# Dictionary setup moved between convolution rounds, and a group norm with one averaging matmul instead of two

## The reference

```
x = x + conv3x3_circular(_gn(x), weight)          # 64 -> 64 channels, written with an FFT
x = x + recon(_gn(x), dictionary)                 # 1024 x 512 dictionary

D = dictionary / (norm of each column + 1e-10)
X = 4x4 patches of all 64 channels                # 1024 numbers a patch, 1024 patches an image
G = D^T D + 1e-5 I;  h_bar = (D^T X)^T;  h = h_bar
for k in 1..5:                                    # greedy pursuit, per patch
    index = argmax |h| over atoms not yet chosen
    extend the Cholesky factor L with G[I, index]
    x_stack = solve(L L^T, h_bar[I])
    h = h_bar - x_stack @ G[I]
recon = D @ coefficients, put back as patches
_gn(v) = (v - mean) / sqrt(var + 1e-5), mean and var over 2 channels and all pixels
```

## Time and profile before

| | |
|---|---|
| three runs | 3581.29, 3585.17, 3589.22 us |
| profiled execution | 3581.48 us, span 3579.5 us |
| busy PE, DVE, ACT, POOL | 3067.3, 2579.2, 2367.6, 1856.7 us |
| start of the first round of the convolution | 80.70 us |
| start of period 1 | 204.83 us |
| start of period 2 | 365.03 us |
| start of period 15 | 3040.45 us |
| mean full period, 2 to 14 | 205.8 us |
| end of the last matmul | 3568.7 us |

### The profile page before, as it was taken

The page is one execution under the profiler, slowest core; times in us unless marked ns, Lnnn a source line. Parts: engine busy times, 40 slices in busy tenths (PEclk is TensorE's granted clock), DMA queues, the critical chain, the costliest instruction groups (busy, mean ns, idle before and its releaser), DMA issues.

```text
span 3579.5 us, 35041 instructions
## 1 busy us (share of the span) xinstructions
PE 3067.3 (86%) x9488; PEld 1310.8 (37%) x9488; DVE 2579.2 (72%) x6596; ACT 2367.6 (66%) x3795; POOL 1856.7 (52%) x1861
## 2 busy tenths in 40 slices
PE   6796889899898989989898989989898998986617
PEld 2232333343333334333333434333333433332303
DVE  2027887878788687878778786878778777887872
ACT  3535686858677676858668685767768576765634
POOL 0015565555555564655656555555655555556651
PEclk8998999999999989999999999999999999997858
DMA  3433443534354343434444353445435344442222
GB/s 114 154 108 117 136 132 97 180 84 145 102 163 132 124 139 91 156 91 154 133 141 131 101 177 73 151 114 158 127 109 163 86 144 102 127 106 60 59 59 47
DMA packets 131028, 428.38 MB, mean 120 GB/s; under 512 B 55696, under 2 KB 55952, under 8 KB 106128
## 3 DMA queue, kind: packets, MB, share of 16 engines
q0 software_dynamic: 91136, 202.10, 23.3%
q1 hardware_dynamic: 39696, 224.05, 17.1%
HBM read 289.70 MB, written 136.31 MB: 119 GB/s over the span
## 4 chain that ended last, share of the span: by engine, by line
PE 49%; DVE 15%; issue 10%; ACT 10%; POOL 8%; DMA 5%; ACTq 0%; POOLq 0%; SPq 0%; DVEq 0%
PE gen_ps L909 22%; PE gen_ps L918 15%; PE conv_ps L952 8%; POOL v L479 7%; DVE u L832 6%; ACT hot L543 4%; PE conv_ps L959 4%; DMA u<-marked_rows,chosen 4%; DVE idx L732 2%; DVE h L840 2%; DVE top L723 2%; ACT score L617 1%; ACT junk_sums L356 1%; ACT ct L530 1%; ACT z L567 1%
## 5 line engine op out<-in xcount | busy, mean ns | idle before, releaser
L479 POOL DMA_INDIRECT v<-gram_rows,cell x1280 | 1278.2, 999 | 919.3 <-DVE cell L741 392.4
L909 PE MATMUL gen_ps<-ct,dt 128*128 128x512 f32 x2048 | 948.1, 618 | 69.6 <-ACT rb L555 60.3
L918 PE MATMUL gen_ps<-dn,z 128*128 128x512 f32 x2048 | 927.9, 607 | 62.4 <-ACT z L567 50.8
L952 PE MATMUL conv_ps<-xh,wc 128*128 128x512 f32 x1536 | 717.1, 617 | 91.0 <-ACT xa L585 83.5
L491 POOL DMA_INDIRECT u<-marked_rows,chosen x504 | 506.1, 1004 | 492.8 <-DVE chosen L737 329.0
L723 DVE MAX8 top<-score 128x8 f32<-128x512 f32 x640 | 420.7, 691 | 294.6 <-ACT score L617 278.5
L909 PEld LDWEIGHTS gen_ps<-ct,dt 128*128 128x128 f32 x2048 | 400.5, 198 | 583.2 <-issue 571.2
L918 PEld LDWEIGHTS gen_ps<-dn,z 128*128 128x128 f32 x2048 | 389.9, 194 | 568.0 <-issue 512.9
L832 DVE SCALAR_TENSOR_TENSOR u<-u,nl 128x512 f32<-128x512 f32 x748 | 514.2, 747 | 95.4 <-DMA u<-marked_rows,chosen 92.6
L617 ACT ACTIVATE score<-h 128x512 f32<-128x512 f32 x640 | 377.6, 604 | 241.3 <-DVE h L840 120.4
L655 DVE SCALAR_TENSOR_TENSOR ce<-hot,xc,ce 128x512 f32<-128x512 f16 x512 | 365.1, 745 | 159.1 <-ACT hot L546 159.1
(11 more groups left out here) (103 smaller groups left out, 1870.5 us busy)
## 6 DMA issues: line engine op xcount, KB each, us to landing
xh<-x_paired SPq DMA_DIRECT2D x128, 650.0 KB, 4.0
xa<-x_pairs SPq DMA_DIRECT2D x64, 1024.0 KB, 6.1
y_rows<-xa SPq DMA_DIRECT2D x64, 1024.0 KB, 6.3
y_rows<-rb POOLq DMA_DIRECT2D x64, 1024.0 KB, 8.3
v<-gram_rows,cell POOLq DMA_INDIRECT x1280
u<-marked_rows,chosen POOLq DMA_INDIRECT x504, 3.8
dn<-atoms SPq DMA_DIRECT2D x1, 2048.0 KB, 7.8
gram_rows<-u SPq DMA_DIRECT2D x4, 256.0 KB, 2.0
```

The costliest lines, as they stand in the source:

```text
L479: pool.indirect_dma_start(v[:, g, k - 1, j, t:t + 1], None, cells, bass.IndirectOffsetOnAxis(ap=cell[:, g, k // (KMAX - 1), j, t:t + 1], a ...
L909: last = pe.matmul(to[:], dt_[:, a, d, :], ct[:, a, :], start=(a == 0), stop=(a == NA - 1))
L918: last = pe.matmul(to[:], z[:, t % 2, d // PATCH, d % PATCH, :], dn[:, d, :], start=(d == 0), stop=(d == ND - 1))
L952: pe.matmul(conv_ps[:, a], wc[:, tap, a * CIN:a * CIN + P], rows[:, a + 1:a + 2 * CP:2, tap:tap + W], start=(tap == 0), stop=False)
```

## The change

1. The group norm needs one matmul. ACT leaves five numbers for each partition instead of two: mean, variance, and the mean with three sign patterns that are loaded as three more columns of `avg`. One matmul (`average`) averages all five over the group. `root` on ACT now has three instructions: the squares of the three signed averages with their sum, that sum added to the averaged variance, and the root. `gn_part` on DVE has five small instructions for the factor in place of nine; `spread` is gone.
2. The setup block loads the first image ahead of the constants, the taps, the first rows and the dictionary (in this order), and only forms the statistics of the first image. ACT waits there for the constants.
3. The dictionary is made ready in period 0: squares on ACT behind the eviction of round 0, norms on PE behind round 1 (`norms`), scaling on DVE before its first period (`normalise_atoms`), Gram blocks 0 and 1 behind rounds 4 and 5, block 2 in front of `average(0, 1)`, block 3 in front of the first correlation, which also waits until block 3 has been copied out. POOL stores both copies of the Gram matrix before its first period. The dictionary is turned in period 1, one piece behind each round, and ACT evicts each piece behind that round's eviction.
4. The tables of the order, PE's written order, and the banks are new for all periods and for the tail.

The diff, cut to what the prediction speaks of:

```diff
-GN_STEPS = 10
-GN_SUMS = (3, 2)
+GN_STEPS = 5
+GN_SUMS = (2, 1)
+GN_ROOT = 3
...
-    1.5: [("co", 0)], 3: [("ce", 0, 0)], 10.5: [("ce", 0, 1)], 23.5: [("co", 1)], 24: [("ce", 1, 0)],
-    30: [("ce", 1, 1), ("gn", 1, 1)], 31: [("gn", 1, 2), ("gn", 1, 3)], 37: [("gn", 0, 1)],
-    39.5: [("gn", 0, 2), ("gn", 0, 3), ("gn", 0, 4)],
+    0.5: [("co", 0)], 3: [("ce", 0, 0)], 10: [("ce", 0, 1)], 24: [("co", 1), ("ce", 1, 0)],
+    30: [("ce", 1, 1), ("gn", 1, 1)], 37.5: [("gn", 0, 1)], 39.5: [("gn", 0, 2)],
...
+    3: [("z", 4), ("oh", 0, 0, 2), ("ev", 0), ("oh", 0, 1, 2), ("oh", 0, 0, 3), ("oh", 0, 1, 3), ("oh", 0, 0, 4),
+        ("oh", 0, 1, 4), ("oh", 0, 2, 1), ("oh", 0, 3, 1), ("z", 5), ("ev", 1), ("ct", 0, 0)],
...
-    (("corr", 4), ("corr", 7), ("re", 0, 2), ("re", 0, 5), ("re", 1, 0), ("corr", 0), ("re", 1, 4), ("re", 1, 6)),
-    (("corr", 5), ("re", 0, 0), ("re", 0, 3), ("re", 0, 6), ("re", 1, 1), ("re", 1, 3), ("re", 1, 5), ("corr", 3)),
-    (("corr", 6), ("re", 0, 1), ("re", 0, 4), ("re", 0, 7), ("re", 1, 2), ("corr", 1), ("corr", 2), ("re", 1, 7)),
+    (("corr", 4), ("corr", 7), ("re", 0, 2), ("re", 0, 5), ("re", 1, 0), ("re", 1, 2), ("re", 1, 4), ("re", 1, 7)),
+    (("corr", 5), ("re", 0, 0), ("re", 0, 3), ("re", 0, 6), ("re", 1, 1), ("re", 1, 3), ("re", 1, 5), ("corr", 2)),
+    (("corr", 6), ("re", 0, 1), ("re", 0, 4), ("re", 0, 7), ("corr", 0), ("corr", 1), ("re", 1, 6), ("corr", 3)),
...
-                               bias=shifted[n][:, 0:1]).then_inc(gn_step[n], 1)
+                               bias=shifted[n][:, 0:1]).then_inc(gn_ready[n], 1)
+                act.activation(mv[:, n, 2:5], avg[:, P:], ACT.Copy, scale=mv[:, n, 0:1]).then_inc(gn_ready[n], 1)
...
+            for a in range(NA):
+                pool.wait_ge(gram_copied, 4 * a + 4)
+                pool.dma_start(gram[a * P:(a + 1) * P, :], u[:, a, 0, :]).then_inc(gram_out, 16)
+                pool.dma_start(marked[a * P:(a + 1) * P, :], u[:, a, 1, :]).then_inc(gram_out, 16)
+            pool.wait_ge(gram_out, 32 * NA)
...
+                    if i == 0 and c == 0:
+                        act.wait_ge(atoms_in, 16)
+                        for d in range(ND):
+                            act.activation(u[:, d // 2, d % 2, :], dn[:, d, :], ACT.Square).then_inc(squared, 1)
+                    elif i == 0 and c == 2:
+                        act.wait_ge(summed, 1)
+                        act.activation(norm[0], gen_ps[2][:], ACT.Sqrt).then_inc(rooted, 1)
+                    elif i == 1:
+                        a, half = divmod(c, 2)
+                        act.wait_ge(turned, c + 1)
+                        act.activation(dt_[:, a, half * 4:half * 4 + 4, :], ct_ps[:], ACT.Copy).then_inc(turned_copied, 1)
...
-                act.wait_ge(gn_step[n], at(image, GN_STEPS, 5))
-                act.activation(gsc[n][:, 4:5], gsc[n][:, 3:4], ACT.Sqrt).then_inc(gn_root[n], 1)
+                gs = gsc[n]
+                act.wait_ge(gn_sum[n], at(image, GN_SUMS[n], 1))
+                act.activation(gs[:, 6:9], st_ps[:, 5 * n + 2:5 * n + 5], ACT.Square, accum_out=gs[:, 0:1]).then_inc(gn_root[n], 1)
+                act.wait_ge(gn_root[n], at(image, GN_ROOT, 1))
+                act.activation(gs[:, 1:2], st_ps[:, 5 * n + 1:5 * n + 2], ACT.Identity, bias=gs[:, 0:1]).then_inc(gn_root[n], 1)
+                act.wait_ge(gn_root[n], at(image, GN_ROOT, 2))
+                act.activation(gs[:, 2:3], gs[:, 1:2], ACT.Sqrt, bias=eps[:, 0:1]).then_inc(gn_root[n], 1)
...
+                    dve.wait_ge(gn_root[n], at(i, GN_ROOT, GN_ROOT))
+                    dve.reciprocal(gs[:, 3:4], gs[:, 2:3]).then_inc(gn_step[n], 1)
+                    after(1)
+                    dve.tensor_scalar(gs[:, 4:5], gs[:, 1:2], GN_EPS, gs[:, 3:4], ALU.add, ALU.mult).then_inc(gn_step[n], 1)
                     after(2)
-                    dve.tensor_tensor(gs[:, 1:2], mv[:, n, 0:1], gs[:, 0:1], ALU.subtract).then_inc(gn_step[n], 1)
+                    dve.tensor_scalar(gs[:, 5:6], gs[:, 4:5], gs[:, 2:3], 0.5, ALU.add, ALU.mult)\
+                        .then_inc(gn_step[n], 1)
                     after(3)
-                    dve.scalar_tensor_tensor(gs[:, 2:3], gs[:, 1:2], gs[:, 1:2], mv[:, n, 1:2], ALU.mult, ALU.add)\
-                        .then_inc(gn_step[n], 1)
-                elif part == 2:
-                    dve.wait_ge(gn_sum[n], at(i, GN_SUMS[n], 2))
-                    dve.tensor_scalar(gs[:, 3:4], st_ps[:, 3 * n + 1:3 * n + 2], GN_EPS, None, ALU.add).then_inc(gn_step[n], 1)
-                elif part == 3:
-                    dve.wait_ge(gn_root[n], at(i, 1, 1))
-                    dve.reciprocal(gs[:, 5:6], gs[:, 4:5]).then_inc(gn_step[n], 1)
-                    after(6)
-                    dve.tensor_tensor(gs[:, 6:7], gs[:, 3:4], gs[:, 5:6], ALU.mult).then_inc(gn_step[n], 1)
-                    after(7)
-                    dve.tensor_scalar(gs[:, 7:8], gs[:, 6:7], gs[:, 4:5], 0.5, ALU.add, ALU.mult)\
-                        .then_inc(gn_step[n], 1)
-                    after(8)
-                    dve.reciprocal(fac[par][:, n, 0:1], gs[:, 7:8]).then_inc(gn_step[n], 1)
-                    after(9)
-                    dve.tensor_scalar(fac[par][:, n, 1:2], gs[:, 0:1], -1.0, fac[par][:, n, 0:1], ALU.mult, ALU.mult)\
-                        .then_inc(gn_step[n], 1)
+                    dve.reciprocal(fac[par][:, n, 0:1], gs[:, 5:6]).then_inc(gn_step[n], 1)
+                    after(4)
+                    dve.tensor_scalar(fac[par][:, n, 1:2], st_ps[:, 5 * n:5 * n + 1], -1.0, fac[par][:, n, 0:1],
+                                      ALU.mult, ALU.mult).then_inc(gn_step[n], 1)
+                    if i == 0 and n == 1:
+                        gram_rows(NA - 1)
...
+            def normalise_atoms():
+                dve.wait_ge(rooted, 1)
+                dve.tensor_scalar(norm[1], norm[0], 1e-20, None, ALU.max).then_inc(inverse, 1)
...
+                for d in range(ND):
+                    dve.tensor_tensor(dn[:, d, :], dn[:, d, :], norm[6], ALU.mult).then_inc(scaled, 1)
...
-            for part in (1, 2, 3, 4):
+            for part in (1, 2):
                 gn_part(0, 0, 0, part)
+            normalise_atoms()
+            for a in range(NA - 1):
+                gram_rows(a)
...
-                if not (img == 0 and n == 0):
+                if img == 0 and n == 0:
+                    pe.wait_ge(turned_copied, 2 * NA)
+                else:
...
+                if i == 0 and t == 0:
+                    gram_block(NA - 1)
+                    pe.wait_ge(gram_copied, 4 * NA - 3)
...
+            def norms():
+                for d in range(ND):
+                    pe.wait_ge(squared, d + 1)
+                    last = pe.matmul(gen_ps[2][:], ones, u[:, d // 2, d % 2, :], start=(d == 0), stop=(d == ND - 1))
+                last.then_inc(summed, 1)
+            def gram_block(a):
+                if a == 0:
+                    pe.wait_ge(scaled, ND)
+                elif a == 3:
+                    pe.wait_ge(gram_copied, 1)
+                for d in range(ND):
+                    last = pe.matmul(gen_ps[a % 3][:], dn[:, d, a * P:(a + 1) * P], dn[:, d, :],
+                                     start=(d == 0), stop=(d == ND - 1))
+                last.then_inc(gram_done, 1)
+            def turn_atoms(n):
+                a, half = divmod(n, 2)
+                if n > 0:
+                    pe.wait_ge(turned_copied, n)
+                for m in range(4):
+                    last = pe.transpose(ct_ps[:, m, :], dn[:, half * 4 + m, a * P:(a + 1) * P], ident[:])
+                last.then_inc(turned, 1)
...
-                pe.wait_ge(gn_step[n], at(i, GN_STEPS, 1))
-                pe.matmul(st_ps[:, 3 * n:3 * n + 1], avg[:], mv[:, n, 0:1], start=True, stop=True).then_inc(gn_sum[n], 1)
-            def spread(i, n):
-                pe.wait_ge(gn_step[n], at(i, GN_STEPS, 4))
-                pe.matmul(st_ps[:, 3 * n + 1:3 * n + 2], avg[:], gsc[n][:, 2:3], start=True, stop=True).then_inc(gn_sum[n], 1)
...
+                if i == 0 and n == 1:
+                    gram_block(2)
+                pe.wait_ge(gn_ready[n], at(i, 2, 2))
+                pe.matmul(st_ps[:, 5 * n:5 * n + 5], avg[:, 0:P], mv[:, n, :], start=True, stop=True).then_inc(gn_sum[n], 1)
...
+                if i == 0 and c == 1:
+                    norms()
+                elif i == 0 and c in (4, 5):
+                    gram_block(c - 4)
+                elif i == 1:
+                    turn_atoms(c)
...
-            spread(0, 0)
...
-            sp.dma_start(dn[:], atoms).then_inc(atoms_in, 16)
+            first_image(sp)
...
-            first_loads(sp)
+            first_rows(sp)
+            sp.dma_start(dn[:], atoms).then_inc(atoms_in, 16)
...
-            act.wait_ge(atoms_in, 16)
-            for d in range(ND):
-                act.activation(u[:, d // 2, d % 2, :], dn[:, d, :], ACT.Square).then_inc(squared, 1)
```

(3 more changed lines are left out.)

184 lines of the change are left out of this document (73 added, 111 removed), and 102 rows, old and new, of tables (SCALAR_PLAN, TAIL_SCALAR_PLAN, TAIL_VECTOR_PLAN).

## The result

| | before | changed |
|---|---|---|
| median of the runs | 3585.17 us | 3595.86 us (3592.53 to 3601.57) |
| ratio to before, 95% interval | | 1.0031 (1.0017 to 1.0044) |
| start of the first round | 80.70 | 41.58 us |
| period 0 | 124.1 | 137.6 us |
| period 1 | 160.2 | 169.5 us |

The kernel got slower, 10.7 us, where 37 us less were forecast. The stretches answer to the earlier trace rows; columns as there (length, busy PE, PEld, DVE, ACT, POOL, clock, DMA share, GB/s).

A forecast was written before the change was run, and what follows sets the result against it. It took a full period as 146.4 us of search on DVE, ACT and POOL, then 58.5 us of PE. Terms -39 + 13 + 8 - 18 - 1 = -37 gave 3548 us; 8 in 10 is 3495 to 3590.

The forecast's parts named there:

- Setup, -39: Before the first round: it starts at 41.7 us against 80.70, so -39 us.
- Period 0, +13: Period 0: norms and four Gram blocks added to PE, partly covered by waits that disappear, +13 us.
- Period 1, +8: Period 1: dictionary turns hide on PE, but round 5's eviction now stands between unit 4's scores, +8 us.
- Full periods, -1.4 each: Thirteen full periods: earlier evictions and rows shorten each by 1.4 us, -18 us in all.
- (a): Full period, ce(0,0): three one-hot pairs now stand in front of eviction 0, -1.4 us.
- (b): Full period, u gather: eviction 3 and the 2 MB store go earlier, so the gather's rows land 2.0 us earlier.
- (c): Full period, against the gains: two sums and a correlation's eviction between unit 5's scores, ACT full from 93 to 111 us.
- (d): End of the full period's search: last sum ends at 142.2 to 143.1 in place of 144.5 us.
- What bounds a period: Full period: 146.4 us of search on DVE, ACT and POOL, then 58.5 of PE; PE waits ahead of 1744 are slack.
- Rival C: Root on ACT, before unit 7's last score, waits for PE's average: slower, +49 us, 3634; chance 0.12.
- The row gather and the store: Full period, u's rows: by the skill's reading they don't stand behind the store; a period would gain only 0.7 us.
- Tail: Last stages: solutions and sums into rows come later, but the ends are gather chains either way, -1 us.

The follow-up runs named there:

- e1c: Changed kernel with the full periods' tables, banks and PE order of the kernel before, new setup, norm and tail kept: 0.9911 of the kernel before, 3549.8 us.
- e7c: Changed kernel, with SyncE's second 2 MB store waiting until POOL's first adding store of the older image has landed: 0.9934 of the kernel before, 3558.4 us.
- e8c: Changed kernel with second store behind the adding store, two loads behind unit 3's cells, root behind unit 7's last score: 0.9860 of the kernel before, 3533.3 us.
- e4: Changed kernel with the root on ACT moved behind unit 7's last score: 1.0000 of the kernel before, 3579.4 us.
- e2b: Changed kernel, with the second 2 MB store of an image waiting for the rows of unit 4: 0.9999 of the kernel before, 3582.4 us.
- e10c: Changed kernel with round 7 and its eviction back behind reconstruction (0,4), no wait added: 0.9925 of the kernel before, 3558.0 us.
- a1: The changed kernel run once more, nothing altered: 1.0029 of the kernel before, full periods 208.5 us.
- e3b: As e2b, and the two loads that follow round 6 wait until unit 3's cells have landed: 0.9989 of the kernel before, 3575.3 us.
- e1: Changed kernel with the order, banks and PE order of the kernel before, tail included: 0.9938 of the kernel before, on the slower kind of chip.
- e8: The same kernel as e8c, run on the slower kind of chip: 1.0026 of the kernel before.
- e1b: The same kernel as e1c, run on the slower kind of chip: 0.9950 of the kernel before.

## Why the prediction was wrong, point by point

- *Setup, -39.* Right: 41.58 against 41.7. ACT began its sums at 13.96 (13.7 was said), the statistics ended at 35.5, and the table of roots was on the path:

```profile
37.15 1.28 ACT L634 ACT_TABLE_LOAD   x1
38.44 0.29 ACT L634 ACTIVATE gsc<-gsc,eps 128x1 f32<-128x1 f32 x1
```

  The root starts 0.01 us behind the load. The further 1.38 us that the Trainium skill ("ScalarE: Activation LUTs", section "What ACT_TABLE_LOAD costs") names as a drain isn't here.
- *Period 0, +13.* Right: 137.59 - 124.1 = +13.5.
- *Period 1, +8.* Right in size, +9.3, and in its cause as far as e1c goes: with the old order the period lasts 161.1. That it is round 5's eviction between the scores wasn't tried alone.
- *Full periods, -1.4 each.* Wrong, +2.7; this term alone turns the forecast's gain into a loss. (a) and (b) came: the rows of unit 1 are worked on 2.2 us earlier. (c) was about right up to unit 5, whose last score ends 1.5 us earlier on average (91.5 against 93.0). What failed is the step from there to (d), the last sum at 142.2 to 143.1 (in the changed kernel it ends at 148.0 in period 8): I carried the gain to the end of the search as if nothing between units 5 and 7 had moved. I had followed the *first* store, which a faster eviction 3 sends earlier, but not the second store and the loads, which rounds 6 and 7, moved up on PE, send 7 and 14 us earlier. They meet the cells of unit 3, the rows of unit 4, the adding store and, behind POOL's queue, the rows of unit 5. Making the store wait gives back 34 us (e7c), and with the loads and the root moved as well 1.0029 - 0.9860 = 1.7%, 59 us (e8c), where these periods had lost 36.
- *What bounds a period.* The step before that one was wrong too. "146.4 us of search on DVE, ACT and POOL" leaves out that 50.9 us of that stretch were PE's (the chain above), so a gain at unit 1 could pass to unit 7 only as far as PE also came sooner, and "a PE wait ahead of 1744 is slack" doesn't hold for the 2.4 us that PE waited for z just ahead of 1680.
- *Rival C, slower by the average.* Its place was near and its mechanism wrong. PE reaches the average at 135.0 us, 7 us later than my walk, and the root stands in front of the last score; but ACT waits there for DVE and for (0,7), not for the average. With the root behind that score (e4) the median is 13 us lower. That the kernel gets slower had 0.12, and the measured 3595.9 us lies outside the range that was given 8 in 10.
- *The row gather and the store.* The Trainium skill ("DMA: Bandwidth & Descriptors", section "Queues, rings and completion order") has each DMA engine take turns between queue rows, packet by packet. The prediction read from it that the store would not hold the rows up. They took 8.53 us beside it and 3.5 to 4.7 us ahead of it (period 13); with the store moved (e2b) DVE's waits for rows halved, and the adding store took 12.5 us with it and 7.9 without. These numbers speak against that reading; whether taking turns alone makes up the difference no run shows.
- *Tail.* -3.1 for -1.

By terms: forecast -39 + 13 + 8 - 18 - 1 = -37; measured, profile against profile, -39.1 + 13.5 + 9.3 + 35.7 - 3.1 = +16.3 (3595.8 - 3579.5).

What stays open: why the eight passes of (0,7) run at the lower clock level in one period and not in the next. In period 13 PE comes to them 1.5 us later than in most and waits 2.2 us and not 5. The wait alone doesn't decide it: in period 2 it was 2.6 us and the passes took 5.37. What sets the level stays open; what it costs is seen in e10c. Of the 3.4 us that unit 7 starts earlier in period 13 than in period 8, 2.1 are those passes and the other 1.4 come from the earlier eviction (0,4). The shares of the store and of the loads, and what the root's place does to the two forms of a period, aren't told apart cleanly either.

## What to carry to other kernels

An engine moved forward sends its stores and loads forward too. For each round or eviction that moves, write down every transfer it releases and what latency-bound gather is in flight at the new time; here one 2 MB store that left 14 us earlier cost 0.95% (e7c against a1), in a kernel whose whole new order cost 1.2%. Before you count a gain at one unit, read the whole chain down to the end, the busy pieces and not only the waits: 51 us of it were PE's here. And a wait that is removed must be followed to the next bound before it is counted: e2b and e3b freed 3 and 5 us at unit 6, and unit 7 started only 1.5 and 1.7 us earlier, since eviction (0,4) then waited longer for its buffer.

## What the hardware showed that was not expected

- A 1 MB adding store, issued within a microsecond of a 2 MB plain store on another queue, landed 12.5 us after its issue (e3b), and 7.9 us without that company (e8c). A gather of 128 rows issued with or just behind such a store took 8.5 and 7.8 us, and 3.5 to 4.7 us ahead of it (the changed kernel, periods 8 and 13).
- On one kind of chip the kernel before took 3889 to 3946 us, 9 to 10% more than on the other, with busy times of DVE and ACT unchanged (2565.5 and 2392.6 us in e1 against 2562.4 and 2387.6 in the changed kernel) and full periods some 25 us longer. In period 8 of e1 there, from 108 to 125 us, PE works 7.2 us, ACT 3.3 and DVE 3.3; in e1c's period 8 on the other kind they work 17.0, 16.5 and 13.6 us in the same stretch. What stops them isn't known. The ranking of versions isn't the same there: e8 is at 1.0026 there and at 0.9860 here, and e1b at 0.9950 and 0.9911.
